# Self attention: transposed row maxima move from bank 6, after the normalized output, to bank 4, one slot earlier

## What is computed

```python
qk = x @ w_attn.T + b_attn
q, k = jnp.split(qk, 2, axis=-1)
q, k, v = (_heads(q), _heads(k), _heads(x))
scores = jnp.einsum('bhqd,bhkd->bhqk', q, k) * scale
scores = jnp.where(causal, scores, -jnp.inf)
y_ar = jnp.einsum('bhqk,bhkd->bhqd', jax.nn.softmax(scores, axis=-1), v)
...
x = _layernorm(x + _L0_attn_ref(x, ...))       # softmax attention + linear attention
x = _layernorm(x + _L0_xattn_ref(ctx_1024, ctx_1024, x, ...))
x = _layernorm(x + _L0_ffn_ref(x, ...))
```

## Time and profile before

| | us |
|---|---|
| three runs | 1770.29, 1775.82, 1775.47 |
| their median | 1775.47 |
| span of the profiled execution | 1773.4 |
| TensorE matmul busy in it | 1681.7 (95%) |
| VectorE busy | 1254.6 (71%) |
| ScalarE busy | 974.2 (55%) |
| GpSimd busy | 1161.8 (66%) |

### The profile page before, as it was taken

The page is one execution under the profiler, slowest core; times in us unless marked ns, Lnnn a source line. Parts: engine busy times, 40 slices in busy tenths (PEclk is TensorE's granted clock), DMA queues, the critical chain, the costliest instruction groups (busy, mean ns, idle before and its releaser), DMA issues.

```text
span 1773.4 us, 30895 instructions
## 1 busy us (share of the span) xinstructions
PE 1681.7 (95%) x10626; PEld 1111.0 (63%) x10626; DVE 1254.6 (71%) x2785; ACT 974.2 (55%) x1939; POOL 1161.8 (66%) x964
## 2 busy tenths in 40 slices
PE   5999999999999989999998999999999999999998
PEld 4766666666666547877863556566565656656566
DVE  5677777777777666767876776877778686777745
ACT  4555555555555443433445565656666665666554
POOL 2556556556555554744565977878788786878874
PEclk9999999999999989999998999999999999999999
DMA  6556555555555464576625543535344354534210
GB/s 199 147 149 168 145 152 156 153 156 165 141 153 153 122 194 152 181 219 185 193 66 155 144 115 88 139 90 155 91 114 114 82 138 99 144 93 108 63 42 31
DMA packets 167273, 237.29 MB, mean 134 GB/s; under 512 B 22087, under 2 KB 73287, under 8 KB 167117
## 3 DMA queue, kind: packets, MB, share of 16 engines
q1 hardware_dynamic: 167116, 235.31, 48.2%
HBM read 91.57 MB, written 41.94 MB: 75 GB/s over the span
## 4 chain that ended last, share of the span: by engine, by line
PE 68%; DVE 12%; POOL 8%; DMA 4%; issue 4%; ACT 2%; SPq 1%; POOLq 0%; DVEq 0%; ACTq 0%
PE bank L1652 9%; POOL cross_added L1974 7%; PE bank L201 5%; PE bank L202 5%; PE bank L203 5%; DVE bank L585 5%; PE bank L1522 5%; PE bank L1490 5%; PE bank L1461 5%; PE bank L369 4%; PE bank L305 4%; PE bank L356 3%; DVE bank L548 2%; PE bank L1558 2%; PE bank L329 2%
## 5 line engine op out<-in xcount | busy, mean ns | idle before, releaser
L1471 DVE TENSOR_REDUCE cross_negmax<-bank 128x1 f32<-128x512 f32 x512 | 338.7, 674 | 149.8 <-PE bank L1461 147.2
L1738 ACT ACTIVATE cpt<-bank 128x512 f32<-128x512 f32 x512 | 297.7, 595 | 143.6 <-PE bank L1490 140.1
L548 DVE CUSTOM_DVE_ANT_0 bank<-bank,future 128x128 f32<-128x128 f32 (+3 forms) x512 | 243.0, 488 | 177.8 <-PE bank L356 177.7
L430 ACT ACTIVATE pt<-bank 128x256 f32<-128x256 f32 (+3 forms) x512 | 217.5, 444 | 260.2 <-PE bank L305 256.1
L1974 POOL TENSOR_TENSOR cross_added<-cross_added,cpt 128x2048 f32<-128x2048 f32 x61 | 280.0, 4591 | 11.5 <-ACT cpt L1738 11.0
L618 POOL TENSOR_SCALAR_AFFINE_SELECT pt<-pt 128x512 f32<-128x512 f32 x128 | 81.1, 634 | 246.8 <-ACT pt L430 246.8
L1490 PE MATMUL bank<-cqk 98*128 98x512 f32 x512 | 227.4, 444 | 7.1 <-ACT cpt L1738 6.2
L1461 PE MATMUL bank<-cqk 96*128 96x512 f32 x512 | 212.5, 418 | 10.7 <-DVE cross_negmax L1471 8.6
L1974 POOL TENSOR_TENSOR cross_added<-cpt,cpt 128x2048 f32<-128x2048 f32 x32 | 146.6, 4581 | 84.0 <-ACT cpt L1738 84.0
L305 PE MATMUL bank<-qk 98*128 98x256 f32 (+2 forms) x512 | 180.6, 359 | 8.4 <-ACT pt L430 3.9
L356 PE MATMUL bank<-qk 96*128 96x256 f32 (+2 forms) x512 | 169.5, 335 | 4.4 <-DMA qk<-stage 4.4
(11 more groups left out here) (207 smaller groups left out, 3623.8 us busy)
## 6 DMA issues: line engine op xcount, KB each, us to landing
qk<-stage SPq DMA_DIRECT2D x384, 128.0 KB, 2.3
cqk<-cstage SPq DMA_DIRECT2D x384, 128.0 KB, 2.3
scratch_memory<-memory SPq DMA_DIRECT2D x32, 512.0 KB, 3.8
ma<-scratch_memory SPq DMA_DIRECT2D x32, 512.0 KB, 3.9
raw<-in_x_t SPq DMA_DIRECT2D x32, 256.0 KB, 2.9
v<-in_x SPq DMA_DIRECT2D x32, 256.0 KB, 3.2
scratch_y_ar<-y_ar SPq DMA_DIRECT2D x32, 256.0 KB, 2.4
my_ar<-scratch_y_ar SPq DMA_DIRECT2D x32, 256.0 KB, 4.6
```

Of the source, the lines that this page charges most:

```text
L548: dve.tensor_tensor_reduce(out=scores, in0=scores, in1=sh.future[:, SEQ - P * (qt + 1):SEQ], scale=-1.0, scalar=-NEG, op0=ALU.add, op1=ALU ...
L1471: dve.reduce_max(s.negmax[gm % 2][:, col:col + 1], max_bank(sh, m)[:, :], AX, negate=True).then_inc(s.dve_max, 1)
L1738: act.activation(s.pt[step % 3][:, j, :], sh.bank[2 + n % 2][:, :], ACT.Exp, scale=SCALE_CROSS).then_inc(s.act_exp, 1)
```

## The change

The transpose of the maxima now stands in slot (2, 1) of TensorE and writes bank 4, which is free between ScalarE's copy in slot (1, 0) and the weighted sums of slot (2, 3). It waits for all maxima of the group and for that copy (`act_raw`). The two readers follow it to slot (2, 2), the store to slot (2, 3), where it stands ahead of the 512 KB store. The first weighted sums of a group now wait for L563 (`dve_sh`), since they overwrite what it reads. The k projection, which used to wait for `dve_sh` on account of bank 6, now waits for `dve_norm`. `LATE_NORM` and `shift_bank` are gone: every group takes its reciprocals in slots (1, 0) to (2, 0).

```diff
--- before.py
+++ after.py
@@ -276,15 +276,6 @@
 PROJECTED = {(0, 0): (2, 7), (0, 1): (2, 8), (0, 2): (2, 9), (0, 3): (2, 10), (1, 1): (2, 11), (2, 0): (3, 0),
              (2, 1): (3, 1), (2, 2): (3, 2), (3, 0): (3, 3), (3, 1): (3, 4), (3, 2): (3, 5), (3, 3): (3, 6)}
-LATE_NORM = NG - 3
-def shift_bank(sh, d):
-    return sh.bank[7 if d > LATE_NORM else 6]
 def self_tensor(pe, s, second, third, cw, sh):
@@ -323,25 +314,17 @@
             pe.wait_ge(s.act_copied, d + 1)
             pe.wait_ge(s.dve_k, min(d + 4, NG))
             if d + 4 > NG:
-                pe.wait_ge(s.dve_sh, min(d + 2, NG))
                 pe.wait_ge(s.dve_norm, NORM * d)
             for jj in range(PER):
                 done = pe.matmul(sh.bank[6][rows_of(jj), :], sh.ones[:, :], s.added[:, jj, :],
                                  start=True, stop=True, skip_group_check=True)
             done.then_inc(s.pe_tot, 1)
-        if kt == 2 and j == 2 and 0 <= g + 1 < NG:
+        if kt == 2 and j == 1 and 0 <= g + 1 < NG:
             d, n16 = g + 1, PER * TILES
             pe.wait_ge(s.dve_max, n16 * (d + 1))
-            if g == LATE_NORM:
-                pe.wait_ge(s.act_k2, 2 * NG - 1)
-            elif g > LATE_NORM:
-                pe.wait_ge(s.dve_sh, g + 1)
-            elif g >= 1:
-                pe.wait_ge(s.dve_norm, NORM * g)
-            else:
-                pe.wait_ge(s.dve_k, g + 3)
-            pe.transpose(shift_bank(sh, d)[0:n16, 0:P], s.negmax[d % 2][:, :], sh.ident[:, :]).then_inc(s.pe_sh, 1)
+            if g >= 1:
+                pe.wait_ge(s.act_raw, g)
+            pe.transpose(sh.bank[4][0:n16, 0:P], s.negmax[d % 2][:, :], sh.ident[:, :]).then_inc(s.pe_sh, 1)
     arrive(pe, sh.self_done)
@@ -365,6 +348,7 @@
         pe.wait_ge(s.v_landed[g % 2], 16 * (g // 2 + 1))
         if g > 0:
             pe.wait_ge(s.act_raw, g)
+        pe.wait_ge(s.dve_sh, min(g + 2, NG))
     for j in range(PER):
         done = pe.matmul(sh.bank[4][rows_of(j), first:SEQ], s.v[g % 2][:, kt, rows_of(j)], pt[:, j, 0:SEQ - first],
                          start=(kt == 0), stop=(kt == TILES - 1), skip_group_check=True)
@@ -389,10 +373,10 @@
                 pe.wait_ge(s.act_k2, 2 * g - 1)
         elif which == K2:
             pe.wait_ge(s.dve_q, 2 * g + 2)
-        elif g >= 2:
-            pe.wait_ge(s.dve_sh, g - 1)
-        elif g == 1:
-            pe.wait_ge(s.dve_k, 1)
+        elif g >= 4:
+            pe.wait_ge(s.dve_norm, NORM * (g - 3))
+        elif g >= 1:
+            pe.wait_ge(s.dve_k, g)
     done = triple(pe, sh.bank[6 if which == K else 7][:, :],
                   (s.w_hi[:, c, col:col + P], s.w_lo[:, c, col:col + P]),
                   (s.xt_hi[b % 2][:, c, :], s.xt_lo[b % 2][:, c, :]), c == 0, c == GROUPS - 1)
@@ -456,12 +440,12 @@
             if g >= 1:
                 act.wait_ge(s.pe_tot, g)
             act.activation(s.added[:, :, 0:P], s.pt[TILES * g % 3][:, :, 0:P], ACT.Copy).then_inc(s.act_copied, 1)
-        if kt == 2 and j == 3 and 0 <= g + 1 < NG:
+        if kt == 2 and j == 2 and 0 <= g + 1 < NG:
             d = g + 1
             act.wait_ge(s.pe_sh, d + 1)
             if d >= 1:
                 act.wait_ge(s.shift_landed[(d - 1) % 3], 32 * ((d - 1) // 3 + 1))
-            act.activation(s.shift[:, 0, :].bitcast(F32R), shift_bank(sh, d)[0:PER * TILES, 0:P],
+            act.activation(s.shift[:, 0, :].bitcast(F32R), sh.bank[4][0:PER * TILES, 0:P],
                            ACT.Copy).then_inc(s.act_sh, 1)
         if kt == 3 and j == 1 and 0 <= g + 3 < NG:
             d = g + 3
@@ -554,16 +538,14 @@
             dve.wait_ge(s.act_k, d + 1)
             dve.scalar_tensor_tensor(out=st[:, 3, :].bitcast(F32R), in0=sh.bank[6][:, :], scalar=bias_column(s, K, d),
                                      in1=st[:, 2, :], op0=ALU.add, op1=ALU.subtract).then_inc(s.dve_k, 1)
-        if 0 <= g - 1 < NG and not LATE_NORM <= g < NG - 1:
+        if 0 <= g - 1 < NG:
             self_norm(dve, s, sh, g - 1, PER * kt + j - PER)
-        if kt == 2 and j == 3 and 0 <= g + 1 < NG:
+        if kt == 2 and j == 2 and 0 <= g + 1 < NG:
             d = g + 1
             hl = s.shift
             dve.wait_ge(s.act_sh, d + 1)
-            dve.tensor_tensor(hl[:, 1, :].bitcast(F32R), shift_bank(sh, d)[0:PER * TILES, 0:P], hl[:, 0, :],
+            dve.tensor_tensor(hl[:, 1, :].bitcast(F32R), sh.bank[4][0:PER * TILES, 0:P], hl[:, 0, :],
                               ALU.subtract).then_inc(s.dve_sh, 1)
-        if LATE_NORM <= g < NG - 1:
-            self_norm(dve, s, sh, g - 1, PER * kt + j - 11)
         if kt == 3 and j == 2 and 0 <= g + 3 < NG:
             d = g + 3
             st = s.stage[d % 2]
@@ -672,6 +654,13 @@
         if kt == 1 and j == 3 and 1 <= g < NG - 1:
             sp.wait_ge(s.pe_pv, TILES * g)
             self_load_v(sp, s, g + 1)
+        if kt == 2 and j == 3 and 0 <= g + 1 < NG:
+            d = g + 1
+            sp.wait_ge(s.act_sh, d + 1)
+            sp.wait_ge(s.dve_sh, d + 1)
+            if d >= 3:
+                sp.wait_ge(s.pe_st, SLOTS * (d - 2))
+            store_shift(sp, s.kq[d % 3], s.shift, s.shift_landed[d % 3])
         if kt == 2 and j == 3 and 0 <= g + 2 < NG:
             d = g + 2
             sp.wait_ge(s.act_k2, 2 * d + 2)
@@ -679,13 +668,6 @@
             if d == 0:
                 sp.wait_ge(s.pool_ones, 4)
             sp.dma_start(t["memory"][d // GROUPS, d % GROUPS][:, 0:2, :], s.memory[:, :, :]).then_inc(s.memory_stored, 16)
-        if kt == 3 and j == 0 and 0 <= g + 1 < NG:
-            d = g + 1
-            sp.wait_ge(s.act_sh, d + 1)
-            sp.wait_ge(s.dve_sh, d + 1)
-            if d >= 3:
-                sp.wait_ge(s.pe_st, SLOTS * (d - 2))
-            store_shift(sp, s.kq[d % 3], s.shift, s.shift_landed[d % 3])
         if kt == 3 and j == 3 and 0 <= g - 1 < NG:
             d = g - 1
             sp.wait_ge(s.dve_norm, NORM * d + NORM)
```

## The result

The changed kernel takes 1788.42 us (median of four runs, 1786.8 to 1791.9). The kernel before, run beside it, has a median of 1772.88 us. The ratio is 1.0099, with a 95% interval of 1.008 to 1.0117: the change makes the kernel 0.8 to 1.2% slower. The forecast was 1789 in a range of 1782 to 1798, and slower. It was worked out from a median of 1775.47 for the kernel before, of three runs; with the fourth that median is 1772.88.

The account below looks back on a forecast made before the run. TensorE's waits were taken to bound the kernel, each group a ring of TensorE's and VectorE's parts. Terms 12.9 - 0.4 + 1 = +13.5 us took the median from 1775.47 to 1789 us, range 1782 to 1798.

Parts of the forecast that it names:

- The bound: Self attention groups: TensorE is busy 1681.7 of 1773.4 us, so a change counts where TensorE itself waits.
- a ring: Each group: TensorE alone from sums to next slot (1, 0), then VectorE alone; any later resumption of sums counts in full.
- The old wait: Transpose's wait for the normalized output goes; TensorE ready for the sums 0.57 us earlier, 16.0 us over 28 groups.
- The new wait: Sums wait for the shift's remainder on VectorE, starting 0.46 us later a group: +12.9 us (11.5 to 13.7).
- The start: k projection in slot (3, 1), group -1, loses its wait for the remainder: -0.4 us (0 to -0.5).
- SyncE: 512 KB store leaves behind the shift's stores; L575, which waits for it, stays covered or nearly so: taken as 0.
- The last groups: Groups 29 and 30, reciprocals ahead of the shift again: sums later, partly absorbed by waiting; +1 us (-1.5 to +4).
- its part for the clock: Last groups: idle time moved ahead of the sums may let the 613.9 to 620.3 stretch run at 2.4 GHz, saving up to 3.
- The sum: Whole kernel: 12.9 - 0.4 + 1 = +13.5 us, span 1773.4 to 1786.9, median 1775.47 to 1789 us.
- the groups' term: Middle groups: 28 x 0.46 = +12.9 us from the sums starting later.
- The rival "covered": Remainder done when TensorE reaches the sums, so only the old wait goes: 1759 us; chance 6%.
- The rival "given back": VectorE's 2.09 us idle time, waiting for TensorE, absorbs the 0.46 us delay: time stays at 1775; chance 6%.

Follow-up runs that it names:

- e7: Changed kernel with transpose, copies and stores back in their old slots, shift still through bank 4; 1817.83 us, ratio 1.0256 to the kernel before.
- e1: Changed kernel with VectorE's remainder of the shift one maximum sooner, at the head of slot (2, 2); 1772.61 us, ratio 1.0015 to the kernel before.
- e2: Changed kernel with the remainder two maxima sooner, directly behind the normalized output in slot (2, 0); 1761.09 us, ratio 0.9953 to the kernel before.
- e3: Changed kernel with the remainder ahead of the normalized output in slot (2, 0), ScalarE's copy in slot (2, 1); 1752.26 us, ratio 0.9907 to the kernel before.
- e4: Changed kernel with the first of a group's four reciprocals taken of one column instead of 128; 1763.45 us, ratio 0.9961 to the kernel before.
- e6: Changed kernel with the reciprocals of groups 29 and 30 behind the shift again, as before; 1790.45 us in one execution.
- e4b: Kernel before with the first reciprocal of a group taken of one column instead of 128; 1752.4 us, ratio 0.9884 to the uncut kernel before.
- e5: Changed kernel with SyncE's old store order in slot (2, 3), 512 KB store ahead of the shift's two; 1790.01 us, ratio 1.0098 to the kernel before.

## Why the prediction was right, step by step

**The bound.** That a group is a ring, in which any later start of the sums goes round in full, is shown from both sides: later starts lengthened it (changed, e7), and earlier ones shortened it (e1, e2, e3, e4). The traces show the two parts as well. From the sums to VectorE's first maximum of slot (1, 0) it is 12.40 to 12.41 us in all eleven kernels (median of groups 5 to 25). The other part, from there to the next sums, is what changed: 6.50 us before, 6.99 in the changed kernel, 6.47, 6.13 and 5.84 in e1, e2 and e3, 7.63 in e7.

**The old wait.** It was put at 0.57 us a group, since TensorE would be ready that much earlier. In e3 neither wait is left ahead of the sums, and the group takes 18.24 us, 0.65 under the kernel before: the mechanism was right, and the size 0.08 low.

**The new wait.** 0.41 to 0.49 us a group, 0.46 taken, because of a wake-up of 0.11 read from the transpose's weight load. Measured are 19.392 - 18.899 = 0.493. The sums' weight load does follow 0.11 behind the remainder, but their first matmul only 0.15: the reading for the matmul, 0.14, was the one to take, the upper bound. From the sums of group 0 to those of group 28 it is 542.97 us against 529.16, so the term is **+13.8**, not +12.9.

**The start.** -0.4 was forecast; the first score product of group 0 (in 50.52 us before) came at 48.55, **-2.0**. The forecast mechanism does not explain that, and one execution each cannot confirm it either. In e6, which is the same program up to group 29, this product starts at 49.30, and in e4, whose cut comes later than group 0's start, at 47.49. So the start differs by 1.8 us between programs that are the same up to there, and most of the -2.0 cannot be told from chance. Part of it goes with the clock: from 39.5 to 48 us its mean is 0.60 in the kernel before and in e7, where the product starts at 50.52 and 50.12, and 0.80 in the changed kernel, e1 and e4b, where it starts at 48.55, 49.09 and 49.09. At like clock the removed wait thus shows 0.4 in one pair (e7, before) and nothing in the other (e1, e4b, which has the order of before).

**SyncE.** 0, right: L557, which was L575, waited for its store twice in the changed kernel, 0.5 us in all, and e5 shows no difference.

**The last groups.** +1 taken of -1.5 to +4; measured +1.1, from group 28 to the last sums. The sums of group 29 came 2.7 us later than the middle groups explain (forecast 2.6). As forecast, TensorE then did not wait for the shift's landing. In group 30 the sums were 1.2 late (forecast 2.1 less what the clock gives back). The clock gave nothing back: from the sums of group 28 to the last ones its mean is 0.80 in both kernels, and the sums of group 29, at the full level before, now run at the lower one (3.21 us instead of 1.71). So the +1 was near, and its part for the clock was wrong.

**The sum.** 13.8 - 2.0 + 1.1 is +12.9; from the last weighted sums on, the changed kernel's profile is 1.3 us shorter, which no part of the change touches and which is inside what such executions differ by (from the last weighted sums to the end it is 1118 to 1127 us in the eleven profiles). That gives the 11.6 us of the two spans, against +13.5 forecast. The medians differ by 15.5, nearer to the 13.8 of the groups and the 1.1 of the last ones. That 1789 lies within 1 us of 1788.42 is partly luck: the kernel before was taken 2.6 us too slow, and the difference 2 us too small. The direction and the mechanism are not luck: the groups' term, the only large one, was right to 0.9 us. The rival "covered" would have needed a remainder 1.0 us sooner; e3 is that case: 17.8 us under the kernel before, where the rival promised 16.4. The rival "given back" did not occur.

## What to carry to other kernels

A wait that is removed from one instruction is only worth what the next wait on the same engine leaves of it; list what the new waiter waits for on its producer's queue, and where in that queue it stands. Here a short operation of 0.27 us decided, for two maxima and a product were queued ahead of it. Moving it ahead of them, with ScalarE's copy one slot sooner so that it was ready, turned a loss of 1.0% into a gain of 0.9%. To find what a group's length depends on, follow each engine back to where it was last idle: the chain between two such places is what can be shortened.

## What the runs showed of the hardware

TensorE's idle time has a second price beyond its own length. With 1.08 us of it at one place in a group of 19.4 us, the granted clock stayed at 1.00 in all middle groups. With 1.74 us in a group of 20.04 us it fell to 0.50 behind the idle time in seven of 28 groups, and each fall added 1.6 us. The Trainium skill (TensorE: Matmul & The Clock Gate, section "A second HAM failure mode: psum-queue depth-cycling") describes such an oscillation from short idle times; by that rule the changed kernel might have shown it and did not, and e7 did, in a quarter of its groups. The two kernels differ in the length of the idle time and in where the transpose stands; what lies between 1.08 and 1.74 us was not run.
